# Positions of three helper steps in the half-position scans: gelu pairs, the sum's copy, the expert block's addition

## The reference, cut to what matters

```python
def step(h, inp):                       # both scans, 16 states n for each channel
    dtt, ut, bt, ct = inp
    dA = jnp.exp(dtt[..., None] * A)
    h = h * dA + (dtt * ut)[..., None] * bt[:, :, None, :]
    y = jnp.einsum('bkdn,bkn->bkd', h, ct)
    return (h, y)
...
h = gelu(jnp.einsum('bsd,edh->ebsh', x, w1) + b1[:, None, None, :], approximate=False)
y = jnp.einsum('ebsh,ehd->ebsd', h, w2) + b2[:, None, None, :]
out = jnp.einsum('bse,ebsd->bsd', masked, y)
```

## Time and profile before

| | us |
|---|---|
| median of 3 runs | 5519.45 |
| lowest and highest | 5518.52, 5521.73 |
| the profiled execution, as timed | 5513.34 |
| its span in the trace | 5511.5 |
| six fused stages, from first to last scan | 710, 345, 709, 348, 713, 345 |

### The profile page before, as it was taken

The page is one execution under the profiler, slowest core; times in us unless marked ns, Lnnn a source line. Parts: engine busy times, 40 slices in busy tenths (PEclk is TensorE's granted clock), DMA queues, the critical chain, the costliest instruction groups (busy, mean ns, idle before and its releaser), DMA issues. The chain is left out here.

```text
span 5511.5 us, 73119 instructions
## 1 busy us (share of the span) xinstructions
PE 4799.4 (87%) x23205; PEld 3436.7 (62%) x23205; DVE 4362.5 (79%) x4529; ACT 3631.4 (66%) x5725; POOL 3954.9 (72%) x3074
## 2 busy tenths in 40 slices
PE   7888797779999987897999988898999988888998
PEld 5766646656666645565766645565666654556777
DVE  6988847858999947987999957896999974996544
ACT  5666455438878857766888857775878865785222
POOL 5888718839999917977999944994999962994121
PEclk9999998989999999998999999998999999999999
DMA  5777606737878706646787824654877752662110
GB/s 202 266 257 261 231 1 238 245 120 275 296 255 291 255 28 208 235 155 234 262 298 264 281 94 157 225 202 162 292 267 278 271 177 90 210 229 92 43 43 29
DMA packets 356677, 1104.83 MB, mean 200 GB/s; under 512 B 33211, under 2 KB 121127, under 8 KB 354873
## 3 DMA queue, kind: packets, MB, share of 16 engines
q1 hardware_dynamic: 356280, 1100.06, 57.3%
HBM read 1086.24 MB, written 13.68 MB: 200 GB/s over the span
## 5 line engine op out<-in xcount | busy, mean ns | idle before, releaser
L1163 PE MATMUL banks<-ident,prod 128*128 128x128 f32 x4752 | 717.6, 289 | 325.0 <-DVE prod L1466 176.4
L1163 PEld LDWEIGHTS banks<-ident,prod 128*128 128x128 f32 x4752 | 576.1, 148 | 602.6 <-DVE prod L1466 308.1
L1457 DVE TENSOR_TENSOR_SCAN banks<-banks,h 128x512 f32<-128x512 f32 x594 | 715.7, 1219 | 143.6 <-ACT banks L1305 106.0
L1408 POOL TENSOR_TENSOR h<-lane,Bb 128x512 f32<-128x512 f32 x576 | 724.4, 1276 | 42.9 <-DMA Bb<-half_rows 31.9
L1305 ACT ACTIVATE banks<-lane,A 128x512 f32<-128x512 f32 x864 | 578.5, 686 | 175.2 <-DVE prod L1466 127.1
L1235 PE MATMUL banks<-w_a,Cb 128*128 128x384 f32 x1536 | 551.7, 488 | 0.0
L1457 DVE TENSOR_TENSOR_SCAN banks<-banks,half_carry_a,h 128x512 f32<-128x512 f32 x396 | 497.8, 1277 | 26.1 <-ACT banks L1305 22.6
L1408 POOL TENSOR_TENSOR h<-half_du_a,Bb 128x512 f32<-128x512 f32 x384 | 482.4, 1275 | 15.2 <-DMA Bb<-half_rows 12.9
L1223 PE MATMUL banks<-big,w_a 128*128 128x256 f32 x1728 | 446.1, 405 | 2.5 <-DMA w_a<-w_in 1.8
L1305 ACT ACTIVATE banks<-half_delta_a,A 128x512 f32<-128x512 f32 x576 | 383.3, 685 | 90.3 <-DVE prod L1466 65.3
L1223 PEld LDWEIGHTS banks<-big,w_a 128*128 128x128 f32 x1728 | 333.9, 201 | 110.3 <-issue 51.8
(11 more groups left out here) (471 smaller groups left out, 12198.7 us busy)
## 6 DMA issues: line engine op xcount, KB each, us to landing
Bb<-half_rows SPq DMA_DIRECT2D x576, 512.0 KB, 4.5
C_first<-rows SPq DMA_DIRECT2D x288, 512.0 KB, 5.4
Cb<-half_rows SPq DMA_DIRECT2D x288, 512.0 KB, 4.3
w_a<-w_in SPq DMA_DIRECT2D x256, 576.0 KB, 6.1
w_b<-w_in SPq DMA_DIRECT2D x128, 576.0 KB, 6.1
half_C_a<-half_rows SPq DMA_DIRECT2D x128, 512.0 KB, 6.6
Bb<-rows SPq DMA_DIRECT2D x96, 512.0 KB, 5.2
half_C_b<-half_rows SPq DMA_DIRECT2D x64, 512.0 KB, 6.8
```

What stands on the lines that cost most here:

```text
L1163: mm = eng.matmul(ps[:, 0, at], src[:, at], m.ident[:, :], start=n == 0 and k == 0, stop=added(s) == (i + 1) * N, is_transpose=True, skip_ ...
L1408: eng.tensor_tensor(m.dBu[:, s % DRIVES, :], m.du[i % 2], m.B[b % BRING][:, cols(s % 2)], ALU.mult).then_inc(st.dbu, 1)
L1457: eng.tensor_tensor_scan(flip(to), flip(slot(s)), flip(m.dBu[:, s % DRIVES, :]), initial, ALU.mult, ALU.add).then_inc(st.scanned, 1)
```

## The change

Three positions move, in the fused stages alone.

1. In layer 0 the first gelu pair of a lane goes from behind decay 8 to behind decay 9, and the third from behind decay 18 (state 2 of the next lane) to behind decay 17 (state 1).
2. `copy_sum` goes from behind decay 3 to behind decay 2, in both layers.
3. `evict` goes from 3 to 4 steps behind the first down of the block's last pair: behind step 9 instead of 8 in layer 0, behind 7 instead of 6 in layer 1. SP's store of the finished tokens moves with it by a step, past one load of B. LAST grows by one where the last block ends a stage.

```diff
-    COPY_AT, BACK_AT, TAKE_AT, SUM_AT, DELTA_AT = 3, 4, 7, 8, 4
+    COPY_AT, BACK_AT, TAKE_AT, SUM_AT, DELTA_AT = 2, 4, 7, 8, 4
...
-    evicts = {pair_at(v, 2) + 3: (v + 1) * 2 // PER - 1 for v in range(PAIRS_IN) if (v + 1) * 2 % PER == 0}
+    evicts = {pair_at(v, 2) + 4: (v + 1) * 2 // PER - 1 for v in range(PAIRS_IN) if (v + 1) * 2 % PER == 0}
...
-                                ((2, 8, 9), (7, 13, 14), (12, 18, 21)), ((0, 6, 7), (4, 9, 10), (8, 13, 12)), out,
+                                ((2, 9, 9), (7, 13, 14), (12, 17, 21)), ((0, 6, 7), (4, 9, 10), (8, 13, 12)), out,
```

## The result

| | before | after |
|---|---|---|
| median (5 runs each on one chip), us | 5519.45 | 5473.17 |
| ratio, 95% interval | | 0.9913, 0.9898 to 0.9928 |
| span of the profiled execution | 5511.5 | 5471.4 |
| stages of layer 0, first to last scan | 710.5, 709.1, 712.2 | 697.1, 694.1, 692.9 |
| stages of layer 1 | 344.9, 347.5, 344.7 | 346.4, 346.2, 345.6 |

The change saves 46 us, 0.87%. The three stages of layer 0 gave 47.7 us in the profiled executions (the sums are 2131.8 and 2084.1); those of layer 1 lost 1.1. All the rest, which the change doesn't touch, was 6 us longer in this execution (2349 against 2343 us). In the profiled executions of all fourteen kernels of this document it lies between 2343 and 2364 us, so sums of stages tell small differences better than whole times.

A forecast was written before the change was run, and what follows sets the result against it. In layer 0's fused stages POOL's work plus its waits for DVE were taken to bound. 14.4 us a stage gave 43 over three, plus 2 in layer 1: 45 us off, 5474 us forecast, range 5441 to 5503.

The forecast's parts named there:

- The border of two lanes: Layer 0, third gelu to decay 17 and copy to decay 2: PE starts each lane 2.1 us earlier, scan 3's 0.38 us go.
- The ceiling by POOL: A layer 0 stage can gain at most the 27.4 us that POOL waits for DVE's scans; 14.4 us forecast.
- The cover of scan 2: At lane borders, gelu start to decay 2's end takes 2.8 us, about 2.9 available; cost 0 to 10 us a stage.
- The gate at the second pair: PE's next up waits for the moved first gelu, some 1 us; covered, but 1 to 2 us in up to 8 lanes.
- Evict a step later: Expert block added behind step 9, not 8: DVE's 8.3 us of waiting for blocks in the first stage go.
- First gelu to decay 9: Layer 0, first gelu pair behind decay 9, not 8: ACT's margin before scan 9 grows from 0.3 to 0.9 us.
- Late scans 2: Scan 2 waiting for its decay in some lanes of layer 0: 2 us a stage taken off the gain.
- The factor of 0.6: Share of POOL's 27.4 us taken as gained, 16.4 us; 22 of DVE's 39 waits for ACT counted as answered.
- the gain stops on POOL: Rival: POOL's own lag leaves a quarter of the 27.4 us, 7 us a stage, 20 in all, 5499 us; chance 0.15.
- PE catches up fully: Rival: waits at scans 14 and 15 and the take go too, 78 us gained, 5441 us; chance 0.13.
- The slower rival: Ups waiting for the first gelu delay projection lanes: 60 us lost, 5579 us, or 5535 with half the gains; chance 0.07.
- The clock: Shorter border waits should remove some of PE's slow stretches; counted only as the reason why PE catches up.

## Why the prediction was right, and where it wasn't

The forecast was 5474 us in a range of 5441 to 5503; measured, 5473. The total is right: its mechanism at the border and PE's catching up are borne out, but the way the gain was shared out isn't, and that the terms add up to the measured total is partly luck.

**What held.** (1) The border of two lanes: PE's first addition was to start 2.1 us earlier; at the border shown it does (5.5 to 3.4 us behind product 15), and the pair of moves that makes it so gives all of the gain. (2) The ceiling by POOL: 14.4 us a stage from a ceiling of 27.4 was forecast, POOL's waits for DVE fell by 14.0 and the first stage by 13.4, the mean stage by 15.9. (3) The cover of scan 2 is thin: nine scans 2 are late, by 8.0 us in all, within the 0 to 10 that the prediction gave; scan 3's waits are gone in return. (4) The gate at the second pair: 12.8 us of PE's waits in 21 places, none over 0.8 us, where "some 1 us" was forecast, and covered as said: with the first gelu back, PE's wait there is 0.4 us, and the kernel is no faster. (5) Layer 1 stayed within 2 us. (6) PE's waits for products rose and its wait for the copy fell to 5.1 us.

**Which step failed.** The prediction shared the gain out among three answers: waits at scan 3, waits at scan 9, and the addition's 8.3 us. The runs give all of it to the two moves at the border. Four parts of the working don't hold:

- *Evict a step later: "The 8.3 us of waiting go".* They go, but this move isn't needed for it. With only the third gelu moved they are 1.4 us, with gelu and copy moved nil. They were a symptom of PE being late, which the prediction itself had said of them before it counted them as an answer of their own. They are also the larger part of what the two moves at the border took from DVE's waits in the first stage: 8.3 us here, and 4.6 at the border itself (9.2 in front of scan 3 before, 4.6 in front of scan 2 with the two moves). Alone, the move is worth 10 us; on top of the other two, nothing.
- *First gelu to decay 9.* The margin of ACT grows: with this move alone the 6.4 us of waiting for the decay in front of scan 9 are gone from the first stage. Worth in time: 1.0000 alone, and nothing on top. In the changed kernel DVE waits for ACT and POOL as long with it as without it (33.4 us), in part for POOL at scan 9, in part at scan 2; and at the second pair PE now waits for the gelu.
- *Late scans 2, taken as 2 us a stage.* They are 8.0 us in the first stage.
- *The factor of 0.6.* It was taken, not worked out, and this is where the luck lies. The count behind it was off as well: the waits before scans 3 and 9 are 28 of the 39 places and not 22 (15.6 of the 26.5 us). And the addition's move and the first gelu's, which it also covers, have no share in the gain.

**The link between two moves.** The prediction put third gelu and copy in one term and never asked what the copy does alone. It is 1.8% slower alone. In front of the gelu the copy makes ACT wait for PE while decay 3 and two table loads are queued behind it. The gelu's move clears the way: it gives 0.53% by itself, and with it the copy's move becomes worth about 0.3% where the other two moves are absent (0.9947 to 0.9913; 16 us in the stages), and 0.1% where they are there (7 us in the stages).

**The rivals.** That the gain stops on POOL (5499) didn't come about, but the run with more work on POOL shows its core of truth: half of what is put on POOL costs time, the other half is taken on without loss, so it isn't the only bound, and waits for transfers share the role. That PE catches up fully was half right: PE has caught up (3.6 us in the stages for the doubled ups), and yet only half of the 27.4 us was gained. The waits before scans 14 and 15, which that rival has going too, remain: 8.8 us in the first stage, before 10.9. The slower rival needed the gate to be long; it is short. Its price "with half the gains" was also mis-added: 60 us of loss less half of 45 give 5557 us, and 5535 is what is left with the whole gain.

**The clock.** It went from 0.95 to 0.98 or 0.99 in the stages of layer 0 in the changed kernel and in the one with two moves, and to 0.96 or 0.97 where only the gelu or all but the copy was moved. With the copy alone it stayed at 0.94 or 0.95, though PE no longer waits for the copy there: its pause comes one instruction later. So the clock goes with the long pauses of PE at the border, whichever instruction they stand before. As more work on PE costs next to nothing now, I take the faster clock to be worth little by itself in the changed kernel; what it was worth while PE was late wasn't tried apart from the waits, so how the gain divides between shorter waits and faster clock stays open.

Open is also how much of the 16 us that remain of DVE's waits for decays could be had: scan 2 is late by up to 1.9 us behind projection lanes and by up to 1.5 behind others, and no run moved the projection.

## What to carry to other kernels

Where several engines wait in a ring, look first for the instruction that waits in front of others in a queue (here the copy on ACT, behind or ahead of a gelu pair with two table loads), and count what is queued behind it; the same move cost 1.8% or gave 0.1 to 0.3%, by what stood behind it. A wait far down the ring may be a symptom: before it gets a term of its own in a sum, ask whether it would be there if the first cause were gone. Here, once PE had caught up, the next gain was in the transfers: two loads of C issued four steps later gave 22 us in the stages of layer 0, and the addition's and the first gelu's moves together none.

## What the runs showed of the hardware that was not expected

Pauses of PE of only 2 to 3 us were followed by slow stretches. At the border into lane 13 PE had waited 2.77 us, and the clock was 0.52 in the next 6 us. Counted in the first fused stage, PE's pauses of 2 us or more and its mean clock are:

| kernel | pauses of 2 us or more | clock |
|---|---|---|
| before | 13 | 0.95 |
| copy alone | 21 | 0.95 |
| third gelu alone | 6 | 0.97 |
| third gelu and copy | 3 | 0.99 |
| changed | 2 | 0.98 |

PE's busy time for the same 3184 instructions fell by 13 us over the stage between the kernel before (655) and the one with two moves (642). This is the row of the latter's first stage:

```profile
1234.00:1930.00 696.00, 641.75 (x3184) 456.12 (x3185) 655.23 (x716) 577.08 (x914) 660.26 (x587) 0.99 0.79 278
```
